# Attention before a mixture of experts: the next head's transposed scores ahead of the second transpose unit

## The reference, cut to what matters

```python
x = x + layernorm(attention(layernorm(x), ...))
x = x + layernorm(moe(layernorm(x), ...))

def attention(hidden, q_w, q_b, k_w, k_b, v_w, v_b, o_w, o_b):
    q = (hidden @ q_w.T + q_b).reshape(b, s, 16, 32)
    k, v = hidden @ k_w.T + k_b, hidden @ v_w.T + v_b          # (b, s, 32)
    scores = einsum('bqhd,bkd->bhqk', q, k) / 32 ** 0.5        # causal
    attn = softmax(where(causal, -inf, scores))
    out = einsum('bhqk,bkd->bqhd', attn, v).reshape(b, s, 512)
    return out @ o_w.T + o_b
```

## Time and profile before

| | us |
|---|---|
| three runs | 2093.07, 2098.26, 2098.34 (median 2098.26) |
| the profiled execution | 2094.07, of which the span from first to last instruction 2092.0 |
| mean granted TensorE clock | 0.962 of full speed |
| matmul records busy | 1961.9 (94% of the span) |

### The profile page before, as it was taken

The page is one execution under the profiler, slowest core; times in us unless marked ns, Lnnn a source line. Parts: engine busy times, 40 slices in busy tenths (PEclk is TensorE's granted clock), DMA queues, the critical chain, the costliest instruction groups (busy, mean ns, idle before and its releaser), DMA issues.

```text
span 2092.0 us, 34929 instructions
## 1 busy us (share of the span) xinstructions
PE 1961.9 (94%) x11932; PEld 1561.9 (75%) x11932; DVE 1150.8 (55%) x2487; ACT 784.2 (37%) x1583; POOL 516.1 (25%) x1105
## 2 busy tenths in 40 slices
PE   4999999999999839989999999998999999999997
PEld 3666666666666427779999999997788888888885
DVE  3566766667665328656777675774532323324234
ACT  2445545455454322245555554553111111111101
POOL 1224334244242324321111111110123022030303
PEclk9799999999999869989999997999999999999999
DMA  5234353453633213356666665765422112131203
GB/s 161 75 112 137 117 188 120 133 149 110 190 117 122 98 60 116 103 169 234 237 241 245 237 237 186 249 240 188 121 82 100 61 60 81 39 120 42 79 20 101
DMA packets 128570, 286.38 MB, mean 137 GB/s; under 512 B 12192, under 2 KB 40864, under 8 KB 119616
## 3 DMA queue, kind: packets, MB, share of 16 engines
q1 hardware_dynamic: 117408, 248.63, 35.3%
q0 software_dynamic: 11040, 36.18, 5.8%
HBM read 205.35 MB, written 76.02 MB: 134 GB/s over the span
## 4 chain that ended last, share of the span: by engine, by line
PE 53%; DMA 1%; DVE 1%; ACT 0%; SPq 0%; issue 0%; POOL 0%; ACTq 0%; POOLq 0%; DVEq 0%
PE sh_bank L1045 19%; PE ex_bank L1045 16%; PE sh_bank L1057 10%; PE ex_bank L1057 8%; PE ex_bank L1607 2%; DMA sh_yk<-shd_in 1%; SPq L1192 0%; SPq L1191 0%; DVE sh_dn L1910 0%; ACT sh_up L1865 0%; DVE sh_up L1910 0%; DVE sh_gate L1910 0%; DMA ys<-sh_yk 0%; ACT sh_dn L1865 0%; DVE sh_stats L129 0%
## 5 line engine op out<-in xcount | busy, mean ns | idle before, releaser
L1045 PE MATMUL ex_bank<-ex_xT,ex_gu 128*128 128x256 f32 (+12 forms) x2808 | 360.3, 285 | 1.0 <-DVE ex_xT L1616 1.0
L1045 PEld LDWEIGHTS ex_bank<-ex_xT,ex_gu 128*128 128x128 f32 (+1 forms) x2808 | 346.4, 186 | 4.8 <-issue 1.2
L1077 DVE TENSOR_TENSOR sh_silu<-sh_silu,sh_bank 128x512 f32<-128x512 f32 x77 | 53.0, 688 | 370.4 <-ACT sh_silu L1070 325.4
L690 DVE TENSOR_REDUCE at_nmax<-at_bank 128x1 fp32r<-128x384 f32 (+3 forms) x512 | 222.4, 477 | 38.2 <-PE at_bank L450 37.6
L886 ACT ACTIVATE at_PT<-at_bank 128x512 f32<-128x512 f32 (+1 forms) x384 | 184.8, 507 | 126.6 <-PE at_bank L463 98.3
L1045 PE MATMUL sh_bank<-sh_xT,sh_gate 128*128 128x512 f32 x924 | 226.9, 395 | 5.3 <-DVE sh_dn L1910 5.3
L1070 ACT ACTIVATE sh_silu<-sh_bank 128x512 f32<-128x512 f32 x77 | 46.1, 598 | 493.3 <-PE sh_bank L1045 477.6
L1045 PE MATMUL sh_bank<-sh_xT,sh_up 128*128 128x512 f32 x924 | 224.7, 392 | 0.0
L1057 PE MATMUL sh_bank<-sh_dn,sh_act 128*128 128x512 f32 x924 | 223.4, 391 | 0.6 <-DVE sh_act L1086 0.6
L1045 PEld LDWEIGHTS sh_bank<-sh_xT,sh_gate 128*128 128x128 f32 x924 | 175.0, 189 | 44.2 <-issue 5.7
L1057 PEld LDWEIGHTS sh_bank<-sh_dn,sh_act 128*128 128x128 f32 x924 | 172.7, 188 | 40.8 <-DVE sh_act L1086 4.4
(11 more groups left out here) (239 smaller groups left out, 2934.7 us busy)
## 6 DMA issues: line engine op xcount, KB each, us to landing
ex_gu_in<-gu_in SPq DMA_DIRECT2D x39, 1408.0 KB
at_Qs<-q_dram SPq DMA_DIRECT2D x96, 256.0 KB, 4.1
ex_dn_in<-dn_in SPq DMA_DIRECT2D x39, 512.0 KB
ys<-sh_yk SPq DMA_DIRECT2D x35, 512.0 KB, 3.1
sh_yk<-x_in SPq DMA_DIRECT2D x16, 1024.0 KB, 5.4
q_dram<-at_q_h SPq DMA_DIRECT2D x64, 256.0 KB, 4.2
xnT<-sh_xT SPq DMA_DIRECT2D x14, 1024.0 KB, 5.8
sh_xT<-xnT SPq DMA_DIRECT2D x14, 1024.0 KB, 7.7
```

The lines of the kernel that those rows point to most:

```text
L690: last = nc.vector.tensor_reduce(nmax[:, s % 2, i:i + 1], S_ps[u][:, col:col + (i + 1) * P], AX_X, ALU.max, negate=True)
L1045: last = self.nc.tensor.matmul(self.gate_up_ps[c % 2][which][0:m, 0:w], cols(i, k), self.xT[j][:, k, 0:w], start=(step == 0), stop=(step = ...
L1077: nc.vector.tensor_tensor(silu[c % 2][0:m, 0:w], silu[c % 2][0:m, 0:w], gate_up_ps[c % 2][1][0:m, 0:w], ALU.mult).then_inc(s["product"], 1)
```

## The change

In the steps of `PAIRED = (2, 3, 9, 10)` TensorE issues `key_scores` between `begin_values` and `second_filler`; before, it issued them at the end of the step. Nothing else is altered: no instruction is added or removed, and the orders of DVE, ACT, POOL and SP stay as they are. `PAIRED` is in force in every turn, so the move is made as well in the four steps without T2.

```diff
                     begin_values(b, s)
-                    if s == 1 and has(n):
+                    if s in (1, *PAIRED) and has(n):
                         key_scores(n, h, head(b, s, 3), keys)
                     second_filler(b, s)
                     end_values(b, s)
                     transpose_v(b, s)
-                    if s not in (1, 14) and has(n):
+                    if s not in (1, 14, *PAIRED) and has(n):
                         key_scores(n, h, head(b, s, 3), keys)
```

## The result

The changed kernel is slower: 2115.82 us in the median of 6 runs (2112.59 to 2121.84) against 2095.66 (2090.85 to 2098.34), a ratio of 1.0102, 95% interval 1.0083 to 1.012. Run again with another three rounds it gave 1.0077 (1.0058 to 1.0095). The profiled execution has a span of 2114.3 against 2092.0.

The account below looks back on a forecast made before the run. TensorE was taken to bound the kernel, matmul records covering 94% of the span. Shifts less removed waits 17.3, plus 1.0, less 1.3, made 17.0 us slower; forecast 2113 us, range 2104 to 2121.

Parts of the forecast that it names:

- The chain from T2 to L433: From transposes T2 through ACT's copy, DVE's low part and DVE's transposed sums to matmul L433: stays 2.69 us.
- The size per step: L433 comes 0.74 us later in each of 26 steps with T2 not itself waiting: 19.2 us in all.
- The hole: TensorE's idle ahead of L433 grows from 0.19 to 0.93 us in 26 places, 24 us in all.
- T2's own wait: TensorE's wait ahead of T2 for DVE's low part, 1.3 us in all, at most 0.3 each, goes.
- The steps without T2: Key scores between the values' 24 and 8 matmuls cost 0.32 us in three of four steps, 1.0 in all.
- Step 11: Key scores there shorten from 1.02 to 0.80 us, giving back 1.3 us over turns 1 to 6.
- the table's last row: Everything up to routing outside the steps listed separately: 0 us change forecast.
- The fill: Rival: filling the holes pays, at best 6.0 us faster, more likely near nothing; chance 0.07 that it pays or costs nothing.
- pays twice: Rival: later T2 makes steps 10 and 3 pay again, some 5 us more; chance 0.05, shared with a single clock fall.
- The clock: Rival: more holes lower TensorE's clock; in each of 13 pairs of steps 39 us more, 2150; chance 0.02.
- The level: Whole kernel: 2111.1 us from the profiled execution, 2115.3 from the median; 2113 chosen between them.

Follow-up runs that it names:

- The third experiment: Against the changed kernel, key scores in the four paired steps stand behind T2 but ahead of the 8 matmuls that end the values: 2099.1 us against 2097.12.
- The fifth: The changed kernel, but in paired steps DVE takes the value bank before it forms T2's low part: 2103.24 us against 2097.05.
- the first experiment: Key scores moved in steps 9 and 10 alone, not in 2 and 3: 2110.94 us against 2097.12 for the kernel before.

## Why the prediction was right, point by point

*The chain from T2 to L433.* Right, and shown: 2.64 long where 2.69 was forecast, T2 2.81 behind the values' start where 2.8 was. The third experiment leaves T2 where it was and the cost is gone. The fifth takes one link out ahead of L433, and L433 waits for nothing; the time then hangs on the chain's other end, the low part.

*The size per step.* 0.68 to 0.69 in steps 9 and 10 instead of 0.74. The forecast held the distance from T2 to L433 fixed at 2.69; behind the key scores T2 takes 0.54 to the next group instead of 0.59, and ACT's copy starts 0.64 behind T2 instead of 0.69. That is the missing 0.05 or so.

*The hole.* I forecast 0.93 idle ahead of L433. From the start of the last masks, the matmuls that end the query scores (337.29 in the timeline), plus the usual 0.10, L433 would have started at 337.39; it starts at 338.22, so 0.83 are lost there, and the other 0.10 in the query scores, which take 0.82 from their start to the last masks (336.47 to 337.29) where they took 0.72 (330.03 to 330.75): behind 32-column matmuls they run slower, inside a wait that would be there anyway. The profile's idle of 0.64 counts from the modelled end of the masks. I named 24 us in 26 places, against 4.1 before. The 4.1 are of the weight loads, and in these it is 20.9; the matmuls' own idle is 8.4 + 8.1 = 16.5. The forecast multiplied a start-to-start figure, 0.93, and held it against an idle of the weight loads, which it had read as TensorE's hole.

*T2's own wait.* Covered, as forecast: none is left of the 1.3, and steps 2 of turns 2 to 6 grew by 0.30 to 0.41 instead of 0.68, 1.6 less in all. Steps 3 have the 0.6 less that was forecast.

*The steps without T2.* 0.33 each, where 0.32 was read from the earlier trace rows. I had taken the fourth at nothing; it pays 0.33, and step 11 behind it gives back 0.23.

*Step 11.* The 0.2 of the earlier trace rows is given back in turns 1 to 6, 1.4.

*What the forecast missed.* The step that fell short is the one on what is given back in step 11. It saw that TensorE's path moves by two shifts and GpSimd's by one, and asked only what wait goes. It didn't ask what else the two paths meet at: DVE's cast hangs on TensorE's path (projection, ACT's scaling, L642), GpSimd's addition on the other, and one step's delay, 0.68, more between them brings the addition from 0.64 behind the cast's start to 0.02 ahead. That cost 4.7 us. The sum in attention still came out (17.0 forecast, 16.9 measured), because the chain was put 2.1 too dear and 2.7 went in the table's last row, forecast as 0; that the two figures are so near is luck, that they are of one size is not.

*The rivals.* The fill covers T2's wait and pays at most that: no gain of any paired step. Nothing pays twice: steps 9 and 10 grew by 0.68 or 0.69 each, turn after turn. The clock: the granted mean was 0.964 after and 0.962 before, and the changed steps have full clock, as have nearly all of turns 1 to 7 on both sides of the loop's stall:

```profile
332.10:338.20 6.10, 5.48 (x55) 3.07 (x52) 4.26 (x14) 2.57 (x6) 0.76 (x2) 1.00 0.01 3
338.20:344.30 6.10, 5.48 (x52) 3.14 (x52) 4.37 (x13) 2.75 (x6) 3.46 (x16) 1.00 0.00 0
82.00:373.00 291.00, 273.07 (x2060) 183.48 (x2052) 188.66 (x434) 139.95 (x306) 99.89 (x258) 1.00 0.41 127
378.00:697.00 319.00, 299.28 (x2263) 199.96 (x2261) 205.68 (x476) 155.38 (x339) 106.11 (x282) 1.00 0.42 134
```

The first two are steps 9 and 10 of turn 3 (stretch, length, busy time of PE, PEld, DVE, ACT and POOL, granted clock, DMA share, GB/s): 5.48 busy of 6.10, clock 1.00.

*The level.* 2113 was forecast from an execution at 2094.07 and a median of 2098.26; the median is 2115.82, inside 2104 to 2121. The distance between the medians was 20.2 in the first comparison and 17.2 in the second, 17.0 forecast; attention accounts for 17 to 18 in both. What the first has beyond that lies behind attention (5.4 in its profiles) and didn't come again.

## What to carry to other kernels

Before work is moved into a wait, ask what the delayed instruction releases, and follow that to the end: here a wait of at most 0.3 was filled with 0.74 of work, and the unit behind it headed a chain over two engines to a wait that was already late. The gain that was really there lay in the order of the engine at the chain's end, which did the work that could wait first and the urgent work behind it: exchanging them brought 2093.44 against 2097.05 in the kernel before, and even with it the move still costs (2103.24). And when two paths shift by different amounts, look at which instructions of theirs use the same resource within about the difference.

## What was not expected of the hardware

A DVE instruction and a GpSimd instruction that both work in the same on-chip memory can exclude each other. The cast L642 (64x512, memory to memory) took 0.42 with GpSimd idle, and 1.54 to 1.59 when GpSimd's addition L1006 (about 1.29) began between 0.02 ahead of it and 0.02 behind; L644, with two inputs in that memory, 0.68 alone and 1.66 to 1.67. The cast's 0.51 to 0.68 in the kernel before are the same thing on a smaller scale: there it began during a mask of GpSimd's (L990, 0.52, in the rows above). In the traces read for this the held cast ended 0.28 after the GpSimd instruction did, behind a mask as behind an addition. Where one begins clearly ahead, the other is held. Where they begin together, a few hundredths of a us decide: with the addition 0.03 behind the cast (turns 2 and 3 of the first experiment) the cast kept its 0.42 and the addition took 1.54; with 0.02 (turns 4 and 5) the cast was held. Reductions out of the matmuls' banks (L690), which also run beside these additions, kept their mean over the kernel, 477 ns before and 476 after. The Trainium skill (SBUF — State Buffer, "Who interferes with whom") says that DVE and GpSimd share one pair of ports as an exclusive lock, that whichever issues first has it for the whole instruction, that casts can take it, and that a DVE instruction with two inputs in this memory contends with a GpSimd instruction that reads it. The trace agrees in who waits, and nearly in how long: 1.29 and 0.42, one behind the other, would make 1.71, and the held cast took 1.54 to 1.59, so some 0.14 of the two overlap.

TensorE's clock: behind the loop's stall of 3.65 to 3.85 the same twelve matmuls took 5.07 and 4.92 in the two profiles of before, and 3.69 and 3.74 in the two of the changed kernel. In the one the granted clock was 0.50 from 364.8 to 371.4 and 1.00 behind that, in the other it was 0.50 from 374.0 to 377.2 only:

```profile
364.80:371.40 6.60, 6.17 (x18) 4.83 (x19) 1.68 (x4) 1.61 (x4) 0.77 (x2) 0.50 0.39 121
...
374.00:377.20 3.20, 3.20 (x12) 2.51 (x13) 1.67 (x4) 1.23 (x4) 0.01 (x1) 0.50 0.23 67
```

So a comparison of two kernels can carry 1.4 us from one place in which no instruction was moved, and a second profile of each need not show it, since each repeated its own length here.
